# Attention 0's rotary embedding and normalisation on VectorE in one block instead of GpSimd

## What is computed

```
x = x + _L0_attn_ref(_layernorm(x), Wq, Wk, Wv, Wo)
x = x + _L0_xattn_ref(ctx_1024, _layernorm(x), ...)   # SSM, 256 channels, 16 states, scan over 256 positions
x = x + _L0_ffn_ref(_layernorm(x), ...)
x = x + _L1_attn_ref(...); x = x + _L1_xattn_ref(...); x = x + _L1_ffn_ref(...)   # the last with 32 experts
```

```
q = q * cos + rotate_half(q) * sin          # the same for k
v = x - mean(x); v * rsqrt(mean(v * v) + 1e-6)   # over a head, for q, k and v
```

## Time and profile before

| | |
|---|---|
| median of 3 runs | 981.01 us (979.77 to 983.08) |
| the profiled execution's own time | 982.47 us |
| its span, first to last instruction | 980.7 us |
| busy: PE / DVE / ACT / POOL | 806.9 / 730.6 / 478.3 / 242.5 us |
| mean granted TensorE clock | 0.914 |

### The profile page before, as it was taken

The page is one execution under the profiler, slowest core; times in us unless marked ns, Lnnn a source line. Parts: engine busy times, 40 slices in busy tenths (PEclk is TensorE's granted clock), DMA queues, the critical chain, the costliest instruction groups (busy, mean ns, idle before and its releaser), DMA issues.

```text
span 980.7 us, 11880 instructions
## 1 busy us (share of the span) xinstructions
PE 806.9 (82%) x3952; PEld 577.3 (59%) x3952; DVE 730.6 (75%) x1083; ACT 478.3 (49%) x990; POOL 242.5 (25%) x162
## 2 busy tenths in 40 slices
PE   6752289897789997698988888889883789999997
PEld 2331165555433464476666665656762579999996
DVE  4889989899975995889899788869947734444443
ACT  2750386462226402466667655656762434544442
POOL 1044300000223021111011021201003446666663
PEclk9685599899789998899999999999996889999999
DMA  4304123232311112011111111011100043434431
GB/s 162 131 23 158 43 86 108 87 104 91 161 32 59 44 64 86 21 44 43 44 44 44 44 43 44 31 54 45 67 0 1 1 155 129 155 134 132 156 130 43
DMA packets 24208, 74.60 MB, mean 76 GB/s; under 512 B 3120, under 2 KB 5696, under 8 KB 23776
## 3 DMA queue, kind: packets, MB, share of 16 engines
q1 hardware_dynamic: 23776, 71.51, 20.5%
q10 hardware_dynamic: 384, 2.49, 0.7%
HBM read 72.55 MB, written 1.44 MB: 75 GB/s over the span
## 4 chain that ended last, share of the span: by engine, by line
PE 47%; DVE 29%; issue 11%; ACT 10%; POOL 2%; DMA 0%; POOLq 0%; DVEq 0%; ACTq 0%; SPq 0%
DVE hS L915 9%; PE ps L1540 6%; PE ps L1654 6%; PE ps L1655 6%; PE ps L1656 6%; DVE hS L907 4%; PE ps L1501 4%; PE ps L1619 3%; PE ps L1520 2%; PE ps L1305 2%; DVE arena L1172 2%; PE ps L1607 2%; ACT dA L546 2%; PE ps L1415 1%; DVE arena L1153 1%
## 5 line engine op out<-in xcount | busy, mean ns | idle before, releaser
L915 DVE TENSOR_TENSOR_SCAN hS<-dA,hS 128x1024 f32<-128x1024 f32 x64 | 157.6, 2462 | 30.2 <-ACT dA L546 29.1
L1278 DVE SCALAR_TENSOR_TENSOR arena<-ps,arena 128x1024 f32<-128x1024 f32 x32 | 39.2, 1225 | 104.1 <-ACT arena L787 94.7
L1305 PE MATMUL ps<-ident,hS 128*128 128x128 f32 x512 | 72.3, 290 | 44.2 <-DVE hS L918 44.1
L1305 PEld LDWEIGHTS ps<-ident,hS 128*128 128x128 f32 x512 | 61.6, 149 | 71.4 <-DVE hS L918 48.8
L1540 PE MATMUL ps<-WB,hT 128*128 128x512 f32 x192 | 88.7, 607 | 3.8 <-DVE arena L1153 2.0
L435 POOL TENSOR_TENSOR MHl<-arena,MHh 128x1024 fp32r<-128x1024 f32 x34 | 81.7, 2403 | 17.2 <-ACT MHh L790 17.2
L546 ACT ACTIVATE dA<-DEL,negA 128x510 f32<-128x510 f32 x128 | 84.8, 718 | 1.7 <-DVE hS L915 1.3
L907 DVE TENSOR_TENSOR hS<-DU,BCb 128x1024 f32<-128x1024 f32 x64 | 84.5, 1320 | 0.1
L1654 PE MATMUL ps<-Wh,MHh 128*128 128x256 f32 x272 | 78.4, 288 | 6.2 <-POOL MHl L435 6.2
L421 POOL TENSOR_SCALAR jst<-jst 128x8 f32<-128x8 f32 x20 | 12.3, 613 | 280.7 <-DVE jst L1161 280.7
L918 DVE TENSOR_TENSOR hS<-hS,BCb 128x1024 f32<-128x1024 f32 x64 | 79.6, 1243 | 2.2
(11 more groups left out here) (220 smaller groups left out, 1900.9 us busy)
## 6 DMA issues: line engine op xcount, KB each, us to landing
BCb<-bc_dram SPq DMA_DIRECT2D x64, 512.0 KB, 3.6
arena<-gate_dram SPq DMA_DIRECT2D x32, 512.0 KB, 3.6
WB<-in_we SPq DMA_DIRECT2D x34, 256.0 KB, 2.7
WB<-in_wqkv SPq DMA_DIRECT2D x1, 3072.0 KB, 12.8
WA<-in_wo ACTq DMA_DIRECT2D x1, 2048.0 KB, 7.5
WA<-in_ffn SPq DMA_DIRECT2D x1, 1408.0 KB, 7.9
pkb<-in_pk SPq DMA_DIRECT2D x2, 698.0 KB, 4.8
X<-in_x SPq DMA_DIRECT2D x1, 1024.0 KB, 7.9
```

The costliest lines, as they stand in the source:

```text
L915: v.tensor_tensor_scan(f(h), f(a), f(h), 0.0, ALU.mult, ALU.add).then_inc(s["scan_done"], 1)
L1305: last = mm(ps[:, ACC_BANK + j // 2, 256 * (j % 2) + P * d:256 * (j % 2) + P * d + P], src[:, d, P * j:P * j + P], ident[:], start=(first ...
```

## The change

The sine products, the addition, the subtraction of the mean and the product with rsqrt go from GpSimd to VectorE, ahead of scan steps 3 to 5 but for the last product, which stands right behind the rsqrt. Scan steps 6 and 7 come after it. On ScalarE the squaring stands behind the decay of step 3 instead of step 6, and the copies of keys and values behind step 7 instead of 9. TensorE accumulates steps 0 to 5 ahead of the attention instead of 0 to 7. The arithmetic is the same.

```
 @@ gpsimd
-            pool.wait_ge(s["qkv0_copied"], NT)
-            pool.wait_ge(ld["rope0"], 32)
-            for hf in range(2):
-                for x in range(2):
...
-                    gp.tensor_tensor(pick(RB, x), pick(QK0, 1 - x), sn.unsqueeze(1).broadcast_to([P, B, H0 + KV0, 16]),
-                                     ALU.mult).then_inc(s["rope0_sin"], 1)
-            pool.wait_ge(s["rope0_sin"], 4)
-            pool.wait_ge(s["rope0_cos"], 1)
-            gp.tensor_tensor(QK0, RA, RB, ALU.add).then_inc(s["rope0_add"], 1)
-            pool.wait_ge(s["rope0_mean"], 1)
-            gp.tensor_tensor(QKV0, QKV0, heads0(st0[:, 0, :]), ALU.subtract).then_inc(s["rope0_rot"], 1)
-            pool.wait_ge(s["rope0_rs"], 1)
-            gp.tensor_tensor(QKV0, QKV0, heads0(st0[:, 2, :]), ALU.mult).then_inc(s["rope0_done"], 1)
             pool.wait_ge(s["rope0_done"], 1)
 @@ scalar
-            steps_to(4)
+            steps_to(3)
             d_u(1)
-            steps_to(6)
             act.wait_ge(s["rope0_rot"], 1)
             sc.activation(SQ0, Q0.rearrange("p t n -> p (t n)"), ACT.Square).then_inc(s["rope0_sq"], 1)
-            steps_to(9)
+            steps_to(7)
             act.wait_ge(s["rope0_done"], 1)
 @@ vector, behind the cosine product
-            for g in range(3, 6):
-                ssm_step(g)
+            for hf in range(2):
+                for x in range(2):
...
+                    v.tensor_tensor(pick(RB, x), pick(QK0, 1 - x), sn.unsqueeze(1).broadcast_to([P, B, H0 + KV0, 16]),
+                                    ALU.mult).then_inc(s["rope0_sin"], 1)
+            dve.wait_ge(s["rope0_sin"], 4)
+            dve.wait_ge(s["rope0_cos"], 1)
+            v.tensor_tensor(QK0, RA, RB, ALU.add).then_inc(s["rope0_add"], 1)
             dve.wait_ge(s["rope0_add"], 1)
             ch.link(v.tensor_reduce(st0[:, 0, :], QKV0, AX.X, ALU.add))
             v.tensor_scalar(st0[:, 0, :], st0[:, 0, :], 1.0 / D0, None, ALU.mult).then_inc(s["rope0_mean"], 1)
-            ssm_step(6)
-            ssm_step(7)
+            dve.wait_ge(s["rope0_mean"], 1)
+            v.tensor_tensor(QKV0, QKV0, heads0(st0[:, 0, :]), ALU.subtract).then_inc(s["rope0_rot"], 1)
+            for g in range(3, 6):
+                ssm_step(g)
             dve.wait_ge(s["rope0_sq"], 1)
...
             last.then_inc(s["rope0_rs"], 1)
+            dve.wait_ge(s["rope0_rs"], 1)
+            v.tensor_tensor(QKV0, QKV0, heads0(st0[:, 2, :]), ALU.mult).then_inc(s["rope0_done"], 1)
...
-            for g in range(8, LAYER_STEPS - 4):
+            for g in range(6, LAYER_STEPS - 4):
 @@ tensor
-            for g in range(8):
+            for g in range(6):
                 acc(g)
             pe.wait_ge(s["rope0_done"], 1)
...
-            step = iter(range(8, LAYER_STEPS))
+            step = iter(range(6, LAYER_STEPS))
```

More of the change, by code:

```diff
@@ L381, in _ @@
             zero_cols(0, 1)
-            pool.wait_ge(s["qkv0_copied"], NT)
-            pool.wait_ge(ld["rope0"], 32)
-            for hf in range(2):
-                for x in range(2):
-                    pick = lambda a, y: tb0(a)[:, :, hf, :].rearrange("p b (n d) -> p b n d", d=D0)[:, :, :, 16 * y:16 * y + 16]
-                    sn = sin0[:, hf, :].rearrange("p (n d) -> p n d", d=D0)[:, :, 16 * x:16 * x + 16]
-                    gp.tensor_tensor(pick(RB, x), pick(QK0, 1 - x), sn.unsqueeze(1).broadcast_to([P, B, H0 + KV0, 16]),
-                                     ALU.mult).then_inc(s["rope0_sin"], 1)
-            pool.wait_ge(s["rope0_sin"], 4)
-            pool.wait_ge(s["rope0_cos"], 1)
-            gp.tensor_tensor(QK0, RA, RB, ALU.add).then_inc(s["rope0_add"], 1)
-            pool.wait_ge(s["rope0_mean"], 1)
-            gp.tensor_tensor(QKV0, QKV0, heads0(st0[:, 0, :]), ALU.subtract).then_inc(s["rope0_rot"], 1)
-            pool.wait_ge(s["rope0_rs"], 1)
-            gp.tensor_tensor(QKV0, QKV0, heads0(st0[:, 2, :]), ALU.mult).then_inc(s["rope0_done"], 1)
             pool.wait_ge(s["rope0_done"], 1)
@@ L989, in _ @@
             v.tensor_tensor(tb0(RA), tb0(QK0), cos0.unsqueeze(1).broadcast_to([P, B, 2, NQK0]), ALU.mult).then_inc(s["rope0_cos"], 1)
-            for g in range(3, 6):
-                ssm_step(g)
+            for hf in range(2):
+                for x in range(2):
+                    pick = lambda a, y: tb0(a)[:, :, hf, :].rearrange("p b (n d) -> p b n d", d=D0)[:, :, :, 16 * y:16 * y + 16]
+                    sn = sin0[:, hf, :].rearrange("p (n d) -> p n d", d=D0)[:, :, 16 * x:16 * x + 16]
+                    v.tensor_tensor(pick(RB, x), pick(QK0, 1 - x), sn.unsqueeze(1).broadcast_to([P, B, H0 + KV0, 16]),
[3 more added lines that the diff above has]
+            v.tensor_tensor(QK0, RA, RB, ALU.add).then_inc(s["rope0_add"], 1)
             dve.wait_ge(s["rope0_add"], 1)
```

## The result

The changed kernel takes **967.52 us** (four runs, 963.13 to 971.37) against 980.68 before on the same chip; the ratio is 0.9854 [0.9821, 0.9887]. Two later comparisons on other chips gave 965.94 against 980.73 and 966.92 against 982.03. The sign and the mechanism were forecast; the size was not: 9.2 us were worked out, 13 to 15 came.

What follows compares the result with a forecast made beforehand. VectorE, standing still beside GpSimd's operations, was taken to bound the stage from 62 to 133 us. 20.6 - 12.7 + (2.76 - 1.4) = 9.2 us saved gave a median of 971.8 us, range 967.5 to 977.

Steps and rivals of the forecast that it cites:

- What bounds the stage: Between 62 and 133 us, layer 0's scan steps 3 to 9: VectorE sets the end, taking turns with GpSimd.
- the 20.6 us of standing still: VectorE's operations stretched beside GpSimd's seven large ones: 20.6 us of waiting should leave VectorE's queue.
- The 12.7 us added: Work moved onto VectorE: sine products 3.0, addition 2.9, subtraction and product 3.4 each; 12.7 us in sum.
- The rival on runs of 16 elements: Sine products on VectorE pay for short operand runs, up to 8.9 us more: gain 0.3, 980.7 us; chance 6%.
- What moves: Reordered stage: steps 3 to 5 follow the block, 6 and 7 the final product, which ends at 102.6 for 121.26.
- The new idle: VectorE waits 1.4 us before step 8's scan for ScalarE's exponential, ready at 114.6; the wait before was 2.76.
- The stage: 9.2 forecast: By step 10's scan, 20.6 - 12.7 + (2.76 - 1.4) = 9.2 us saved; it starts at 124.05 instead of 133.28.
- all 9.2 should reach the end: Behind the stage nothing has a fixed time, so the whole 9.2 us come off: 982.47 becomes 973.2 when profiled.
- the rival on the attention's start: TensorE's lower clock through transposes and scores adds up to 5 us idling before scan 8: 976 us; chance 7%.
- the low ends of the added operations: Cheapest costs for the operations moved to VectorE, 12.0 us in sum: 0.7 us more saved, 971.1 us.
- the stretch as a property of the stage: Transfers or ScalarE, not GpSimd, lengthen VectorE's operations: 20.6 us stay, 12.7 come on top, 993.7 us; chance 4%.
- All GpSimd time was stall: GpSimd's whole 30.85 us would be freed on VectorE instead of 20.6: saving 19.5, 961.5 us; chance 3%.

Runs made afterwards that it cites:

- e6: Changed kernel with the subtraction and the last product given back to GpSimd, VectorE not waiting for them: 973.36 us, ratio 0.9923 to the kernel before.
- e7: Changed kernel with the subtraction and last product back on GpSimd and VectorE waiting for them, so nothing runs beside them: 971.33 us, ratio 0.9894 to before.
- e3: Kernel before with only the engine of the seven GpSimd operations changed to VectorE, each at its old place: 965.92 us, ratio 0.9867.
- e4: Changed kernel with three more reductions over the heads on VectorE ahead of the subtraction: 981.66 us, ratio 0.9999 to the kernel before.
- e14: Kernel before with twelve unused products on TensorE, misplaced behind the accumulation of step 31: 989.15 us, ratio 1.0095 to the kernel before.
- e13: Changed kernel with twelve unused products on TensorE, misplaced behind the accumulation of step 31: 980.37 us, ratio 0.9997 to the kernel before.
- e2: Changed kernel with ScalarE's decays of steps 8 and 9 issued ahead of its wait for the last product: 968.83 us, ratio 0.9880 to before.
- e16: Kernel before with six unused products on TensorE in its pause ahead of the accumulation of step 31: 978.51 us, ratio 0.9968 to the kernel before.
- e9: Changed kernel with nine unused products on TensorE in each of its two pauses ahead of the experts: 969.09 us, ratio 0.9870 to before.

## Why the prediction was right and where it was wrong

- **What bounds the stage, and the 20.6 us of standing still: right.** All stretched rows went back to 2.29 and 1.22. e6 and e7 show the cause, which the profile of before had only suggested.
- **The 12.7 us added: right.** Sine products 3.02, addition 2.83, subtraction and product 3.36 each: 12.6. The rival on runs of 16 elements falls. The final product ended at 103.09 for 102.6, and the stretch had begun 0.46 later.
- **What moves: right, and of no weight.** e3 gives the same stretch without it.
- **The new idle:** 1.04 for 1.4. TensorE met a better clock in the transposes than in the execution of before.
- **The stage: 9.2 forecast.** 9.14 by step 10's scan in the two profiles, 9.6 from the start of the stretch.
- **"I find nothing with a fixed time on the way, so all 9.2 should reach the end": this step failed.** In place of equality there is a further term of about 4 to 5 us, with its own spread of up to 8 us from run to run. The low stretches of TensorE's clock don't keep their distance to the instructions: 5.3, 25.8 and 53.1 us behind step 30's scan in one execution, 8.3 and 28.8 in another. Between those two, 2.6 us were traced to named matmuls; for the rest of the term the clock is argued from e4, from the pair e14 and e13, and from the single runs' clocks. The page of before had the hint, in tenths over 40 slices of 24.5 us:

```profile
PEclk9685599899789998899999999999996889999999
```

Behind the stage (from the seventh slice on) there are still slices of 6 to 8 tenths. I read the clock only for the rival on the attention's start. That rival looked for it inside the stage, and it was to cost time; it came behind the stage, and gave some.
- **The range:** the low ends of the added operations lead to 971.1, and the step from there to 967.5 has no term behind it. There was none for the clock of the later stages, and the edge, 0.986 of the time before, lay just above what was measured three times, 0.985.
- **The rivals:** the stretch as a property of the stage, and no gain from the sine products, are excluded. "All GpSimd time was stall" is excluded by the rows, which show 20.6; that the total came out about halfway between it (961.5) and the forecast (971.8) says nothing for it.

**Open:** why the kernel before holds the slow values in nearly every run while the changed one changes between them; whether the changed order of work has a hand in that; and how the extra 4 to 5 us of the median divide over the later stages.

## What to carry to other kernels

Before work is spread over VectorE and GpSimd, look for VectorE rows of one form with two durations and lay GpSimd's operations beside them: two-operand work of the two took turns here, so 12.6 us of it on VectorE replaced 30.85 on GpSimd that had cost VectorE 20.6. A local edit's worth is best read as a stretch between two fixed instructions, which repeated here to 0.1 us while totals of one and the same kernel spread by 8. A change that moves everything behind it by some microseconds gets a further term of either sign, here mostly from TensorE's clock as far as it was traced: of some 5 us, as large as half the saving, so a range should be open to it on both sides.

## What the runs showed of the hardware that was not expected

- GpSimd and VectorE on two-operand work gain next to nothing from overlap: 0.5 us an operation on VectorE's queue and nothing in the stretch, 66.36 us with it, 65.98 with VectorE idling. GpSimd's 3072 elements took 5.36 us alone, 6.27 beside a product that had started just before, VectorE's own 3.36.
- 1.02 us taken out at 115 us (e2) left the median 1.3 to 2.9 us higher; 10.0 put in (e4) raised it by 14.1 to 15.7, though its two groups of runs are some 4 us apart.
- Unused matmuls made a kernel faster: six of them (5.3 us of TensorE's time in a pause) took 2.8 us off the kernel before (e16). The same idea at the experts removed 20.5 us of low clock for 1.3 us (e9).
